# Expert products in exponential buffers, Gelus read from PSUM in even tiles, and the first group's Gelus in the attention's end

## The chip, the cores and the metric

The kernel runs on one core of one Trainium2 chip. The metric is the device time of the whole kernel in microseconds, the median of several runs. PE is the TensorE, DVE the VectorE, ACT the ScalarE, POOL the GpSimd engine, SP the engine that issues most DMAs.

## The reference

```python
x = L0_attn_x                                   # 16 x 512 x 128, f32
x = x + attn(layernorm(x), w_qkv, w_proj)       # 16 heads of 8, window +-128
x = x + ffn(layernorm(x), gamma, beta, w_q, keys, key_in, key_out)

def ffn(inputs, ...):                           # 8192 rows of 128
    xn = batchnorm(inputs) * gamma + beta
    q = xn @ w_q.T                              # 2 halves x 8 heads x 128
    sim = einsum('pbnhd,hkpd->pbnhk', q, keys)  # 2 x 8 heads x 32 keys
    # top 8 of each half, top 8 of their 64 sums: idx into 1024 experts, scores
    o = einsum('bnd,bnhkd->bnhk', inputs, key_in[idx])
    o = gelu(o, exact) * softmax(scores)
    return einsum('bnhk,bnhkd->bnd', o, key_out[idx])
```

## The kernel before

The program has two stages, one after the other, each with hand-written instruction streams for PE, DVE, ACT, POOL and SP that meet at semaphores. The first is the attention of 16 sequences with the layer norm after it; it writes x1 (the residual stream) and x2T (the normed rows, transposed) to DRAM and gathers the batch norm's statistics. The second is the FFN.

**FFN.** 8192 rows are 16 groups of four tiles of 128 rows; k is the tile in its group (0 to 3), so k = 0 and 2 are even tiles and k = 1 and 3 odd ones, and j counts all 64 tiles. The FFN doesn't gather experts. For each tile and each of 8 heads it builds all 1024 pair sums (POOL, L820, into a ring of 16 buffers SUM), takes the exponential of each less a bias (ACT, L947, into PSUM), masks with "at least the eighth best" (DVE, L1054, into W), and adds the transposed weights of the eight heads in the PSUM tile WT (PE, L1125, eight transposes a head). One head of a tile, LH = 3, goes another way: ACT shifts it (L903) and takes its exponential with the mask in it (L909), without DVE; it is called the log head below. Then DVE multiplies WT with the Gelus of the expert products (CT, L1034) and PE multiplies CT with key_out, the output product (L1086, L1089).

Exponentials have two PSUM buffers E of 128 x 1024: an exponential waits until the mask two before it is done. MB is one PSUM bank that passes between PE and ACT: the similarity product of tile j+3 (L1064, copied by ACT to SIM, L853), the output product of tile j-1 (copied to OUT, L873), and the expert products of the next group, key_in times X2T (L1067), two in a tile, each copied by ACT to GE (L864). Where the slots stand in the loop over heads h is set by SLOT_A, SLOT_OUT, SLOT_SIM, SLOT_B (PE) and COPY_B, COPY_A, COPY_OUT, COPY_SIM (ACT). After head 3 of tiles 2 and 0 ACT runs one Gelu over four products in GE (`gelus`, L859), with a table load before and one after (L859, L860).

The choice of the best eight of the next tile is DVE's small work, `choose`, in parts: 0 to 3 rank SIM's keys, 4 and 5 build and rank candidates, 6 is the sum Z of the small exponentials (L1007), 7 the biases NL and NB; 8 and 9 build the log head's pair sum on DVE for tiles 1 and 3. EVEN_PARTS and ODD_PARTS say which part stands before which head's mask. ACT adds `small_exp` (L890) after head 5, `small_ln` (L894) after head 6, and in tile 1 the batch-normed rows `bnt` (L868, before head 2's exponential).

At the FFN's start PE and ACT make the first group's eight expert products and Gelus (L1077, L881), with the first similarity product between them, and then the next two similarity products.

**Attention.** Step c works on the scores of sequence c, the exponentials of c-1, the values and projection of c-2, and the transposes of the second norm of c-3; each step is a loop over 16 heads. In step 17 (c == SEQS + 1) only the last values, the attention transposes (ASLOT, through MB one after the other), the projection and one X2T are left. MB's users come in the order of the list SHARED, and `bank_free` waits for the one before. SP's queue reloads x1 and x2T of sequence 0 for the FFN in step 17.

Of the kernel before, what the change touches and what calls it, by code (L numbers as in the profile page):

```python
# [52 lines left out]
def attention(nc, ctx, x, w_qkvT, w_projT, identb, band, bands, w_q, keysT, idf, bnst, KM, extra, x1_out, x2T_out, first):  # L53
# [6 lines left out]
    def sem(name):  # L60
# [56 lines left out]

    names = ("waits_passed max_parts_stored memory_loaded keys_merged keys_copied consts_loaded "
# [7 lines left out]
             "x1_stored x2T_stored x_stats x_means sums_inverted x1_stats x1_means first_loaded").split()  # L126
# [45 lines left out]
    def _(sp):  # L172
# [30 lines left out]
        def step(t, c):  # L203
            if 0 <= c - 2 < SEQS:
                if c - 3 >= 0:
                    await_(sp, S["x1_ready"], t - 2)
                sp.dma_start(xres[:, :, :], xs[t - 2]).then_inc(S["residual_loaded"], 16)
# [28 lines left out]
            if 0 <= c - 2 < SEQS:  # L236
                if c == SEQS + 1:
                    x1_first, x2T_first = first
                    sp.wait_ge(S["x1_stored"], 16)
                    sp.dma_start(x1_first[:, :, :], x1s[0]).then_inc(S["first_loaded"], 16)  # L240
                    sp.wait_ge(S["x2T_stored"], 16)
                    sp.dma_start(x2T_first[:, :], x2Ts[0]).then_inc(S["first_loaded"], 16)
                await_(sp, S["x1_ready"], t - 1)
                sp.dma_start(x1s[t - 2], X1[:, :, :]).then_inc(S["x1_stored"], 16)
# [53 lines left out]
    def _(act):  # L298
# [3 lines left out]
        def step(t, c):  # L302
            b = c % 2
            for h in range(H):
# [12 lines left out]
                if h == 3 and 0 <= c - 3 < SEQS:  # L317
# [79 lines left out]
    def _(dve):  # L397
# [41 lines left out]
        def step(t, c):  # L439
            b = c % 2  # L440
            for h in range(H):
# [58 lines left out]
                for i, sl in enumerate(ASLOT):  # L500
                    if h == sl and 0 <= c - 2 < SEQS:
                        n = (t - 2) * 2 + i + 1
                        dve.wait_ge(S["att_turned"], n)
                        hv = MB[:, :, :].rearrange("p g (h e) -> p (g h) e", e=SLOT_V // 2)
# [19 lines left out]
    def _(pe):  # L524
# [74 lines left out]
        def step(t, c):  # L599
            b = c % 2  # L600
            for h in range(H):
# [24 lines left out]
                if h == 3 and 0 <= c - 3 < SEQS:  # L626
# [24 lines left out]
                for i, sl in enumerate(ASLOT):  # L651
                    if h == sl and 0 <= c - 2 < SEQS:
                        bank_free(pe, f"att{i}", t, c)
                        pe.wait_ge(S["values_copied"], (t - 1) * 2)
                        for n in range(4):
                            k = 2 * i + n // 2
                            o = pe.transpose(MB[:, n, :], U[b][:, n % 2, k * P:(k + 1) * P], idf[:, :])
# [6 lines left out]
                if h == 14 and 0 <= c - 2 < SEQS:  # L664
# [3 lines left out]
                    o.then_inc(S["projected"], 1)  # L668

# [21 lines left out]
LH = 3  # L691
# [6 lines left out]
SIM0 = 2  # L698
SLOT_A, SLOT_OUT, SLOT_SIM, SLOT_B = 0, 2, 4, 6
COPY_B, COPY_A, COPY_OUT, COPY_SIM = 1, 3, 5, 7  # L700


def ffn(nc, ctx, x1, x2T, KM, key_in, key_out, gb, ident, bnst, first, out):
# [6 lines left out]
    def sem(name):  # L710
# [14 lines left out]
    GE = [sb(f"GE{b}", [P, BLK, GN]) for b in range(2)]  # L725
# [25 lines left out]
             "experts_weighted out_product out_copied expert_product expert_copied gelu_ready "  # L751
# [64 lines left out]

    def pair_sums(eng, j, h, q):
# [31 lines left out]
    def _(act):  # L849
# [26 lines left out]
        nc.scalar.preload_act_table_set("gelu_and_others")  # L876
        for e in range(BLK):
            if e == SIM0:
                sim_copy(0, 0)
            act.wait_ge(S["expert_product"], e + 1)  # L880
            nc.scalar.activation(GE[0][:, e, :], E[e // 2 % 2][:, e % 2 * GN:(e % 2 + 1) * GN], ACT.Gelu).then_inc(S["expert_copied"], 1)  # L881
        act.wait_ge(S["expert_copied"], BLK)
        act.sem_inc(S["gelu_ready"], 2)
        nc.scalar.preload_act_table_set("natural_log_exp_and_others")
        sim_copy(1, 1)
        sim_copy(2, 2)
# [27 lines left out]
        def group(g, b, more):  # L914
            for k in range(GT):
# [4 lines left out]
                for h in range(FH):  # L920
                    if h == 0:
                        act.wait_ge(S["bias_ready"], j + 1)

# [3 lines left out]
                    if h == COPY_B and k and more:  # L927
                        o_copy(g + 1, 1 - b, 2 * k - 1)
                    if h == COPY_B and not k and real:
                        o_copy(g, b, BLK - 1)  # L930
                    if h == COPY_A and more:
                        if k == 0:
                            wait_pos(act, S["experts_weighted"], g * GT)
                        o_copy(g + 1, 1 - b, 2 * k)
                    if h == COPY_OUT and (real or k):
# [17 lines left out]
                    if (k, h) == (2, 3) and more:  # L953
                        gelus(g + 1, 1 - b, 0)
                    if (k, h) == (0, 3) and real:
                        gelus(g, b, 1)
# [5 lines left out]
    def _(dve):  # L962
# [98 lines left out]
    def _(pe):  # L1061
# [4 lines left out]
        def o_block(b, e):  # L1066
# [123 lines left out]
```

## Time and profile before

| | us |
|---|---|
| median of three runs | 1676.41 (1676.0 to 1678.02) |
| the profiled execution | 1682.29 |
| its span, first to last instruction | 1680.5 |
| attention with its end | to about 715 |
| FFN | from about 715 to 1678 |

Spans and busy times are read as microseconds; a row of a timeline has start, duration, engine, line, operation, and in brackets the idle time of the engine before it and what ended it. Instructions of ACT and DVE that follow each other overlap by about 0.1 us, so a row of two is shorter than twice one.

### The profile page before, as it was taken

The page shows a single profiled execution, that of the slowest core. Times are in us where ns is not written, and L with a number is a line of the kernel's source. Part 1 is how long each engine was busy: PE and PEld are TensorE (multiplying, and loading weights), DVE is VectorE, ACT ScalarE, POOL GpSimd, SP SyncE. Part 2 cuts the span into 40 slices and gives each one's busy share as a digit, 9 for nine tenths or more (in the row PEclk, how much of TensorE's full clock was granted, in tenths as well). Part 3 has the DMA queues.
Part 4 walks back from the last instruction along what each step waited for, and adds up shares of the span by engine and source line. Part 5 has one row for each costly group of instructions (what it writes and reads, how often), then busy time and mean ns, then how long its engine had stood idle before and what let it go on. Part 6 is the DMA issues. An engine that isn't in the chain of part 4 may idle for free.

```text
span 1680.5 us, 33160 instructions
## 1 busy us (share of the span) xinstructions
PE 1473.9 (88%) x10688; PEld 1015.7 (60%) x10688; DVE 1477.5 (88%) x4616; ACT 1315.6 (78%) x1805; POOL 1269.8 (76%) x1547
## 2 busy tenths in 40 slices
PE   4799999999999999688888888888888888888887
PEld 2355555555555554356666767767676676767766
DVE  4789999999999996269999999999999999999997
ACT  1266666666666666479999999999999999999995
POOL 1055555556556555389999999999999999999992
PEclk7599999999999999789999999999999999999999
DMA  6344444554445551100000000000000000000000
GB/s 158 82 91 106 113 106 112 119 113 110 108 108 115 111 107 39 44 20 1 20 20 20 1 20 20 1 20 20 8 12 20 20 2 20 20 5 16 14 7 7
DMA packets 73629, 86.39 MB, mean 51 GB/s; under 512 B 9872, under 2 KB 63760, under 8 KB 68752
## 3 DMA queue, kind: packets, MB, share of 16 engines
q1 hardware_dynamic: 72840, 82.70, 20.7%
q10 hardware_dynamic: 616, 1.57, 0.5%
q8 instruction: 85, 1.39, 0.4%
q14 instruction: 88, 0.72, 0.2%
HBM read 58.30 MB, written 25.95 MB: 50 GB/s over the span
## 4 chain that ended last, share of the span: by engine, by line
ACT 21%; DVE 16%; PE 11%; issue 10%; DVEq 0%; ACTq 0%; SPq 0%
DVE W L1054 10%; ACT E L947 10%; PE WT L1125 7%; ACT L860 2%; ACT L859 2%; ACT W L909 2%; PE MB L1064 2%; PE MB L1067 2%; ACT SIM L853 1%; DVE SMALL L1000 1%; DVE M8Y L983 1%; ACT GE L859 1%; ACT GE L864 1%; PE E L1077 1%; DVE Z L1007 0%
## 5 line engine op out<-in xcount | busy, mean ns | idle before, releaser
L820 POOL TENSOR_TENSOR SUM<-SIM 128x1024 f32<-128x1024 f32 x480 | 899.5, 1910 | 34.2 <-DVE W L1054 30.8
L1125 PEld LDWEIGHTS WT<-idf,W 128*128 128x128 f32 x4096 | 478.6, 147 | 211.7 <-issue 126.4
L1054 DVE SCALAR_TENSOR_TENSOR W<-SUM,SMALL,E 128x1024 f32<-128x1024 f32 x448 | 560.6, 1280 | 42.6 <-ACT E L947 42.1
L1125 PE MATMUL WT<-idf,W 128*128 128x128 f32 x4096 | 545.4, 284 | 56.8 <-DVE CT L1034 38.0
L268 POOL TENSOR_SCALAR_AFFINE_SELECT PT<-PT 128x128 f32<-128x128 f32 (+1 forms) x1024 | 335.2, 353 | 266.5 <-ACT PT L371 230.8
L947 ACT ACTIVATE E<-SUM,NB 128x1024 f32<-128x1024 f32 x448 | 495.4, 1116 | 20.5 <-DVE W L1054 17.5
L430 DVE CUSTOM_DVE_ANT_0 SY<-SY,bandf 128x384 f32<-128x384 f32 x512 | 273.4, 574 | 0.0
L371 ACT ACTIVATE PT<-TX 128x512 f32<-128x512 f32 x256 | 153.1, 598 | 116.3 <-PE TX L565 116.1
L451 DVE TENSOR_REDUCE mx<-SX 128x2 f32<-128x512 f32 x256 | 174.6, 682 | 58.9 <-PE SX L547 58.8
L373 ACT ACTIVATE PT<-TY 128x768 f32<-128x768 f32 x256 | 207.6, 811 | 4.1 <-PE TY L565 0.4
L593 PE MATMUL PV<-PT,V 128*32 128x384 f32 (+1 forms) x2048 | 166.8, 444 | 2.6 <-POOL PT L268 2.4
L537 PE MATMUL SY<-K,Q 72*128 72x384 bf16 x512 | 145.1, 342 | 8.6 <-DVE mx L430 4.7
L1064 PE MATMUL MB<-KM,BNT 128*128 128x512 f32 x128 | 76.7, 683 | 72.7 <-ACT OUT L873 70.9
L565 PE MATMUL TY<-Q,K 75*128 75x384 bf16 x512 | 128.3, 333 | 11.3 <-ACT PT L373 10.2
L1089 PE MATMUL MB<-KO,CT 128*128 128x128 f32 x1024 | 124.9, 275 | 1.1 <-DVE CT L1034 1.1
L537 PE MATMUL SX<-K,Q 72*128 72x256 bf16 x512 | 103.0, 283 | 19.9 <-issue 9.3
L1089 PEld LDWEIGHTS MB<-KO,CT 128*128 128x128 f32 x1024 | 119.5, 192 | 1.3 <-DVE CT L1034 1.3
L565 PE MATMUL TX<-Q,K 75*128 75x256 bf16 x512 | 101.3, 280 | 2.4 <-ACT PT L371 2.0
L565 PEld LDWEIGHTS TX<-Q,K 75*128 75x128 bf16 x512 | 38.4, 99 | 97.7 <-issue 84.0
L593 PEld LDWEIGHTS PV<-PT,V 128*32 128x32 f32 x2048 | 53.8, 110 | 68.8 <-issue 50.0
L1034 DVE TENSOR_TENSOR CT<-WT,GE 128x1024 f32<-128x1024 f32 x64 | 78.4, 1225 | 12.7 <-PE WT L1125 12.7
L537 PEld LDWEIGHTS SX<-K,Q 72*128 72x128 bf16 x512 | 49.2, 100 | 63.3 <-DVE mx L451 14.6
(121 smaller groups left out, 1858.6 us busy)
## 6 DMA issues: line engine op xcount, KB each, us to landing
Q<-q_parts SPq DMA_DIRECT2D x288, 64.0 KB
K<-k_parts SPq DMA_DIRECT2D x90, 192.0 KB
q_parts<-qp SPq DMA_DIRECT2D x16, 384.0 KB, 2.4
k_parts<-kp SPq DMA_DIRECT2D x15, 384.0 KB, 2.4
xin<-in_x SPq DMA_DIRECT2D x16, 256.0 KB, 3.2
xres<-in_x SPq DMA_DIRECT2D x16, 256.0 KB, 9.5
x<-X SPq DMA_DIRECT2D x16, 256.0 KB, 2.2
x2T<-X2T SPq DMA_DIRECT2D x16, 256.0 KB, 2.1
```

The costliest lines, as they stand in the source:

```text
L268: return nc.gpsimd.affine_select(out=out, in_=out, compare_op=ALU.is_ge, fill=0.0, base=0, pattern=([[0, 2]] if pairs else []) + [[s, P]], ...
L373: nc.scalar.activation(pt[:, 512:1280].rearrange("p (j n) -> p j n", j=2), TY[:, :, 0:384], ACT.Exp).then_inc(S["inner_exp"], 1)
L430: return nc.vector.tensor_tensor_reduce(out=scores, in0=scores, in1=bandf[:, k0 * P:k1 * P], scale=1.0, scalar=-3e38, op0=ALU.add, op1=ALU ...
L451: nc.vector.tensor_reduce(mx[:, h, 0:4:3], SX[:, :, :], AX.X, ALU.max).then_inc(S["outer_maxima"], 1)
L537: return pe.matmul(out, Q[b][0:KQ, h, i * P:(i + 1) * P], K[b][0:KQ, h, k0 * P:k1 * P], start=clear, stop=done, skip_group_check=True)
L565: return pe.matmul(out[:, 0:(q1 - q0) * P], K[b][0:R, h, j * P:(j + 1) * P], Q[b][0:R, h, q0 * P:q1 * P], start=True, stop=True, skip_grou ...
L593: o = pe.matmul(PV[32 * e:32 * e + 32, q0 * P:q1 * P], V[b][:, slot:slot + SLOT_V], PT[:, h % 8, at:at + (q1 - q0) * P], start=(j == 0 and ...
L820: return eng.tensor_tensor(SUM[(q * FH + h) % RING][:, :].rearrange("p (i j) -> p i j", i=NK), sx, sy, ALU.add)
L947: nc.scalar.activation(E[(n - 1) % 2][:, :], SUM[(k * FH + h) % RING][:, :], ACT.Exp, bias=NB[q][:, h:h + 1]).then_inc(S["exp_ready"], 1)
L1054: nc.vector.scalar_tensor_tensor(out=W[h % WRING][:, :], in0=SUM[(k * FH + h) % RING][:, :], scalar=TOP[q][:, h, TOPK - 1:TOPK], in1=E[(n ...
L1089: o = pe.matmul(po, CT[k % 2][:, e, :], key_out[:, e, :], start=False, stop=(e == BLK - 1))
L1125: o = pe.matmul(WT[:, e, :], W[h % WRING][:, e * P:(e + 1) * P], ident[:, :], is_transpose=True, start=(h == 0 and e % 4 == 0), stop=(h == ...
```

## The change

- **Expert products.** They leave MB. In the even tiles, four products at a time go into the two exponential buffers (`expert_bank`), a pair after mask 0 and a pair after mask 1, and ACT's Gelu reads them from PSUM, one by one, and writes GE. The copies L864 are gone. k = 2 makes the first four of the next group, k = 0 the last four of its own.
- **Order in a tile.** The log head is 2 instead of 3. The output product stands at head 2 in even tiles and at head 0 in odd ones (SLOT_OUT), its copy at 4 and 5. The small work moves to before mask 3 in even tiles and from head 4 to head 5 (parts 4 and 5) in odd ones.
- **The first group.** Its eight products and Gelus move to step 17 of the attention, into the score buffers SY and TY, at heads 0, 9 and 14. For that the loads of sequence 0 move to step 16 on SP, the X2T transposes and copy of step 17 move from head 3 to 8, and the second attention transposes go to SX, right behind the first.

```diff
+    def first_bank(e):
+        return (SY if e // 2 % 2 == 0 else TY)[:, e % 2, :]
+    def att_bank(i, c):
+        return SX[:, :, :].rearrange("p j (i n) -> p (j i) n", n=P) if i == 1 and c == SEQS + 1 else MB[:, :, :]
+    FIRST = ((0, 0, 2), (9, 2, 4), (14, 4, 8))
...
         def step(t, c):
+            if c == SEQS:
+                sp.wait_ge(S["x1_stored"], 16)
+                sp.dma_start(first[0][:, :, :], x1s[0]).then_inc(S["first_loaded"], 16)
+                sp.wait_ge(S["x2T_stored"], 16)
+                sp.dma_start(first[1][:, :], x2Ts[0]).then_inc(S["first_loaded"], 16)
...
-                if h == 3 and 0 <= c - 3 < SEQS:
+                if h == (8 if c == SEQS + 1 else 3) and 0 <= c - 3 < SEQS:
...
+                for hh, e0, e1 in FIRST:
+                    if h == hh and c == SEQS + 1:
+                        if e0 == 0:
+                            nc.scalar.preload_act_table_set("gelu_and_others")
+                        for e in range(e0, e1):
+                            act.wait_ge(S["first_product"], e + 1)
+                            nc.scalar.activation(first[2][:, e, :], first_bank(e), ACT.Gelu).then_inc(S["first_gelu"], 1)
...
-                    if h == sl and 0 <= c - 2 < SEQS:
-                        bank_free(pe, f"att{i}", t, c)
+                    if h == (ASLOT[0] if c == SEQS + 1 else sl) and 0 <= c - 2 < SEQS:
+                        if i == 1 and c == SEQS + 1:
+                            pe.wait_ge(S["outer_maxima"], SEQS * H)
+                        else:
+                            bank_free(pe, f"att{i}", t, c)
...
+                for hh, e0, e1 in FIRST:
+                    if h == hh and c == SEQS + 1:
+                        pe.wait_ge(S["first_loaded"], 32)
...
+                        for e in range(e0, e1):
+                            if e >= 4:
+                                pe.wait_ge(S["first_gelu"], e - 3)
+                            pe.matmul(first_bank(e), first[3][:, e * P:(e + 1) * P], first[1][:, :], start=True, stop=True).then_inc(S["first_product"], 1)
...
-LH = 3
+LH = 2
-EVEN_PARTS = ((), (), (), (), ((1, 0), (1, 1), (1, 2), (1, 3), (1, 4), (1, 5), (1, 8), (2, 0), (2, 1), (1, 9)), (), ((1, 6),), ((1, 7),))
-ODD_PARTS = ((), (), ((1, 2),), ((1, 3),), ((1, 4), (1, 5)), (), ((1, 6),), ((1, 7),))
-SLOT_A, SLOT_OUT, SLOT_SIM, SLOT_B = 0, 2, 4, 6
-COPY_B, COPY_A, COPY_OUT, COPY_SIM = 1, 3, 5, 7
+EVEN_PARTS = ((), (), (), ((1, 0), (1, 1), (1, 2), (1, 3), (1, 4), (1, 5), (1, 8), (2, 0), (2, 1), (1, 9)), (), (), ((1, 6),), ((1, 7),))
+ODD_PARTS = ((), (), ((1, 2),), (), ((1, 3),), ((1, 4), (1, 5)), ((1, 6),), ((1, 7),))
+SLOT_OUT, SLOT_SIM = (2, 0), 4
+COPY_OUT, COPY_SIM = (4, 5), 7
...
+    def expert_bank(j, e):
+        return E[(j * MASKED + e // 2) % 2][:, e % 2 * GN:(e % 2 + 1) * GN]
...
-        def gelus(g, b, half):
-            act.wait_ge(S["expert_copied"], g * BLK + (half + 1) * 4)
-            o = GE[b][:, 4 * half:4 * half + 4, :].rearrange("p e n -> p (e n)")
-            nc.scalar.activation(o, o, ACT.Gelu).then_inc(S["gelu_ready"], 1)
+        def gelus(j, g, b, half):
+            wait_pos(act, S["experts_weighted"], (g - 1) * GT)
+            nc.scalar.preload_act_table_set("gelu_and_others")
+            for e in range(4 * half, 4 * half + 4):
+                act.wait_ge(S["expert_product"], g * BLK + e + 1)
+                nc.scalar.activation(GE[b][:, e, :], expert_bank(j, e), ACT.Gelu).then_inc(S["expert_copied"], 1)
             nc.scalar.preload_act_table_set("natural_log_exp_and_others")
+            act.wait_ge(S["expert_copied"], g * BLK + 4 * half + 4)
...
+        def o_blocks(j, g, b, half, h):
+            if half == 0:
+                pe.wait_ge(S["x2T_loaded"], (g + 1) * 16)
+            pe.wait_ge(S["weights_masked"], masked(j, h))
+            for e in range(4 * half + 2 * h, 4 * half + 2 * h + 2):
+                pe.matmul(expert_bank(j, e), key_in[:, e * P:(e + 1) * P], X2T[b][:, :], start=True, stop=True).then_inc(S["expert_product"], 1)
...
                 for h in range(FH):
+                    for hh, after in ((0, 0), (2, 1)):
+                        if h == hh and k == 2 and more:
+                            o_blocks(j, g + 1, 1 - b, 0, after)
+                        if h == hh and k == 0 and real:
+                            o_blocks(j, g, b, 1, after)
-                    if h == SLOT_OUT and real:
+                    if h == SLOT_OUT[k % 2] and real:
```

## Rows read from the trace of the kernel before

**Rows 1.** Busy us (count) by stretch: PE, PEld, DVE, ACT, POOL; PE's granted clock.
```profile
728.50:1678.00 949.50, 819.77 (x5610) 657.73 (x5610) 876.64 (x2658) 878.71 (x1055) 890.95 (x476) 0.96 0.04 13
1002.45:1061.62 59.17, 51.37 (x355) 41.08 (x354) 55.00 (x170) 55.77 (x67) 57.36 (x32) 0.97 0.05 14
1066.30:1069.70 3.40, 3.39 (x11) 2.21 (x12) 3.40 (x4) 3.21 (x6) 2.33 (x2) 0.53 0.01 2
694.30:697.50 3.20, 3.17 (x20) 1.31 (x20) 1.11 (x4) 0.00 (x0) 0.94 (x1) 0.51 0.15 44
```

**Rows 2.** Groups of instructions from 720 us to the end, costliest first.
```profile
L820 POOL TENSOR_TENSOR SUM<-SIM 128x1024 f32<-128x1024 f32 x480 | 899.5, 1910 | 34.2 <-DVE W L1054 30.8 <-ACT SIM L853 3.2
...
L864 ACT COPY GE<-MB 128x512 f32<-128x512 f32 x120 | 70.0, 583 | 6.4 <-PE MB L1067 6.4
...
L859 ACT ACTIVATE GE<-GE 128x2048 f32<-128x2048 f32 x30 | 57.5, 1916 | 0.3
...
L881 ACT ACTIVATE GE<-E 128x512 f32<-128x512 f32 x6 | 3.6, 597 | 1.6 <-PE E L1077 1.6
```

**Rows 3.** DVE in order of time, one even and one odd tile.
```profile
1024.81 2.48 DVE L1054 SCALAR_TENSOR_TENSOR W<-SUM,SMALL,E 128x1024 f32<-128x1024 f32 x2 [0.37 <-ACT E L947]
1027.29 1.23 DVE L1034 TENSOR_TENSOR CT<-WT,GE 128x1024 f32<-128x1024 f32 x1
...
1030.81 0.85 DVE L983 MAX8 SMALL<-SIM 128x8 f32<-128x32 f32 x8
...
1036.67 2.49 DVE L1054 SCALAR_TENSOR_TENSOR W<-SUM,SMALL,E 128x1024 f32<-128x1024 f32 x2 [0.53 <-ACT E L947]
1039.08 0.21 DVE L1007 TENSOR_REDUCE Z<-E 128x8 f32<-128x64 f32 x1
...
1041.07 2.48 DVE L1054 SCALAR_TENSOR_TENSOR W<-SUM,SMALL,E 128x1024 f32<-128x1024 f32 x2 [0.38 <-ACT E L947]
...
1048.11 0.22 DVE L990 TENSOR_TENSOR CD<-SMALL,M8Y 128x64 f32<-128x64 f32 x1
...
1049.77 2.47 DVE L1054 SCALAR_TENSOR_TENSOR W<-SUM,SMALL,E 128x1024 f32<-128x1024 f32 x2
...
1054.14 1.29 DVE L1054 SCALAR_TENSOR_TENSOR W<-SUM,SMALL,E 128x1024 f32<-128x1024 f32 x1 [0.37 <-ACT E L947]
```

**Rows 4.** ACT in order of time, the same two tiles.
```profile
1029.83 1.15 ACT L909 ACTIVATE W<-SUM,NL 128x1024 f32<-128x1024 f32 x1
1031.00 1.28 ACT L859 ACT_TABLE_LOAD   x1
...
1034.22 1.28 ACT L860 ACT_TABLE_LOAD   x1
1035.52 1.12 ACT L947 ACTIVATE E<-SUM,NB 128x1024 f32<-128x1024 f32 x1
...
1039.91 2.16 ACT L947 ACTIVATE E<-SUM,NB 128x1024 f32<-128x1024 f32 x2
...
1043.52 0.81 ACT L868 ACTIVATE BNT<-X2T_first,ab 128x512 f32<-128x512 f32 x1
```

**Rows 5.** Line 1007 over the FFN, one Z for each tile.
```profile
L1007 DVE TENSOR_REDUCE Z<-E x64: 210/211/220, 729.0 to 1658.3; 128x8 f32<-128x64 f32 x64
```

**Rows 6.** PE in order of time, in two even tiles.
```profile
1011.57 1.02 PE L1067 MATMUL MB<-X2T,KI 128*128 128x512 f32 x2
1012.43 1.91 PE L1125 MATMUL WT<-idf,W 128*128 128x128 f32 x16
...
1066.31 2.04 PE L1064 MATMUL MB<-KM,BNT 128*128 128x512 f32 x2 [2.37 <-ACT OUT L873]
```

**Rows 7.** The attention's end and the FFN's start in order of time.
```profile
698.95 0.59 ACT L356 COPY U<-PV 128x512 f32<-128x512 f32 x1 [0.66 <-PE PV L593]
...
719.32 0.58 ACT L853 COPY SIM<-MB 128x512 f32<-128x512 f32 x1 [0.26 <-PE MB L1064]
...
729.85 2.15 ACT L947 ACTIVATE E<-SUM,NB 128x1024 f32<-128x1024 f32 x2 [0.35 <-DVE NB L1011]
```

More of the change, by code:

```diff
@@ L236, in step @@
             if 0 <= c - 2 < SEQS:
[L237 to L242, printed above, removed]
                 await_(sp, S["x1_ready"], t - 1)
@@ L625, in step @@
                     o.then_inc(S["xn_turned"], 1)
-                if h == 3 and 0 <= c - 3 < SEQS:
+                if h == (8 if c == SEQS + 1 else 3) and 0 <= c - 3 < SEQS:
                     bank_free(pe, "x2T", t, c)
@@ L724, in ffn @@
     BNT = [sb(f"BNT{b}", [P, GN]) for b in range(2)]
-    GE = [sb(f"GE{b}", [P, BLK, GN]) for b in range(2)]
+    GE = [first[2], sb("GE1", [P, BLK, GN])]
     OUT = [sb(f"OUT{b}", [P, GT, P]) for b in range(2)]
@@ L873, in finish @@
             nc.scalar.copy(OUT[b][:, k, :], MB[:, 0:P]).then_inc(S["out_copied"], 1)
[L876 to L883, printed above, removed]
+        act.sem_inc(S["expert_copied"], BLK)
         nc.scalar.preload_act_table_set("natural_log_exp_and_others")
+        sim_copy(0, 0)
         sim_copy(1, 1)
-        sim_copy(2, 2)
         def small_exp(j):
@@ L922, in group @@
                         act.wait_ge(S["bias_ready"], j + 1)
+                    if h == 1 and j == 0:
+                        sim_copy(2, 2)
                     if h == 2 and k == 1 and more:
                         bnt(g + 1, 1 - b)
[L927 to L935, printed above, removed]
+                    if h == COPY_OUT[k % 2] and (real or k):
                         finish(j - 1, *((g, b, k - 1) if k else (g - 1, 1 - b, GT - 1)))
@@ L942, in group @@
                         l_exp(j, k, q)
+                        if k == 2 and more:
+                            gelus(j, g + 1, 1 - b, 0)
+                        if k == 0 and real:
+                            gelus(j, g, b, 1)
                     else:
@@ L952, in group @@
                         small_ln(j + 1)
[L953 to L956, printed above, removed]
         steps(act, group)
@@ L1064, in similar @@
             pe.matmul(MB[:, :], BNT[b][:, k * P:(k + 1) * P], KM[:, :], start=True, stop=True).then_inc(S["sim_product"], 1)
-        def o_block(b, e):
-            pe.matmul(MB[:, :], key_in[:, e * P:(e + 1) * P], X2T[b][:, :], start=True, stop=True).then_inc(S["expert_product"], 1)
-        for e in range(BLK):
-            if e == SIM0:
-                pe.wait_ge(S["bn_rows"], 1)
-                similar(0, 0, 0)
-            pe.wait_ge(S["x2T_loaded"], 16)
-            if e >= 4:
-                pe.wait_ge(S["expert_copied"], e - 3)
-            pe.matmul(E[e // 2 % 2][:, e % 2 * GN:(e % 2 + 1) * GN], key_in[:, e * P:(e + 1) * P], X2T[0][:, :],
-                      start=True, stop=True).then_inc(S["expert_product"], 1)
-        for k in (1, 2):
-            pe.wait_ge(S["sim_copied"], k)
+        def o_blocks(j, g, b, half, h):
[4 more added lines that the diff above has]
+                pe.matmul(expert_bank(j, e), key_in[:, e * P:(e + 1) * P], X2T[b][:, :], start=True, stop=True).then_inc(S["expert_product"], 1)
+        pe.sem_inc(S["expert_product"], BLK)
+        pe.wait_ge(S["bn_rows"], 1)
+        for k in range(3):
+            if k:
+                pe.wait_ge(S["sim_copied"], k)
             similar(k, 0, k)
@@ L1096, in group @@
                 for h in range(FH):
-                    if h == SLOT_A and more:
-                        pe.wait_ge(S["x2T_loaded"], (g + 2) * 16)
-                        pe.wait_ge(S["sim_copied"], j + 3)
-                        pe.wait_ge(S["expert_copied"], (g + 1) * BLK + 2 * k)
-                        o_block(1 - b, 2 * k)
-                    if h == SLOT_OUT and real:
+                    for hh, after in ((0, 0), (2, 1)):
[4 more added lines that the diff above has]
+                    if h == SLOT_OUT[k % 2] and real:
                         pe.wait_ge(S["sim_copied"], j + 3 if more or k < 2 else GROUPS * GT)
-                        pe.wait_ge(S["expert_copied"], (g + 1) * BLK + (2 * k + 1 if more else 0))
                         wait_pos(pe, S["out_copied"], j - 1)
@@ L1109, in group @@
                         pe.wait_ge(S["bn_rows"], (g + 1) if k < 1 else (g + 2))
-                        pe.wait_ge(S["expert_copied"], (g + 1) * BLK + (2 * k + 1 if more else 0))
                         wait_pos(pe, S["out_copied"], j)
                         similar(j + 3, b if k < 1 else 1 - b, (k + 3) % GT)
-                    if h == SLOT_B and more:
-                        pe.wait_ge(S["sim_copied"], j + 4)
-                        o_block(1 - b, 2 * k + 1)
                     if h == LH:
@@ L1146, in program @@
         bnst = sb("bnst", [P, SEQS, 6])
-        first = [sb("X1_first", [P, TILES, P]), sb("X2T_first", [P, T])]
+        first = [sb("X1_first", [P, TILES, P]), sb("X2T_first", [P, T]), sb("GE_first", [P, BLK, T]), KI]
         extra = [(idf[:, :], ident), (KI[:, :], key_inT), (KO[:, :, :], key_out), (GB[:, :], gb)]
```

19 lines of the change are left out of this document (10 added, 9 removed).

## The prediction

> **What bounds the kernel now.** I read the busy times by stretch first. Over the FFN, ACT is busy 879 us, DVE 877, POOL 891 and PE 820 of 949.5; in one period of four tiles (59.17 us) ACT is busy 55.8, DVE 55.0 and PE 51.4 [rows 1]. No engine is full, so the waits between them count. POOL makes 30 pair sums in a period (480 in 16), 1.874 us each (899.5 / 480), so 56.2 us: a floor that no saving on ACT can pass [rows 2].
>
> Then I read one even and one odd tile in order of time. Both are measured from M, the start of the mask of head 7 of the tile before. The even tile runs from M = 1024.81 to 1041.07 (16.26 us), the odd one to 1054.14 (13.07) [rows 3]. In the even tile ACT runs without a gap: the log head's exponential at M+5.02, table load M+6.19, Gelu, table load back M+9.41, exponential M+10.71 [rows 4]. DVE, which has its small operations from M+6.00 to M+11.33, waits 0.53 us for that exponential [rows 3]. Then Z starts at 1039.08, and from Z to the next mask of head 7 it is always 1.99 us (log, copy of SIM, exponential), in either kind of tile. From the first Z to the last it is 63 tiles in 929.3 us [rows 5]. 29 of the even tiles take 16.25 to 16.50, the other three 13.92, 15.77 and 14.55; that leaves 929.3 - 44.2 - 471.5 = 413.6 for 31 odd tiles, 13.34 each.
>
> **What leaves ACT.** Eight copies of 0.583 go, and two Gelus of 1.916 become eight of 0.597 [rows 2]. A copy and the next instruction overlap by 0.10, so one copy is 0.48 of ACT's time and one small Gelu 0.49: 8 x 0.48 + 2 x 1.92 - 8 x 0.49 = 3.8 us per period off ACT. The table loads stay four, 1.28 each [rows 4]. ACT had 3.4 us of gaps in a period already [rows 1], so the saving counts only where ACT is late for DVE. That is the even tile.
>
> **The even tile, worked out.** Exponential 7 starts at M-1.16, since the mask needs it. Exponentials follow each other by 1.04 (two in 2.16 [rows 4]): exponential 0 M-0.12, shift M+0.92, exponential 1 M+1.96, log head M+3.00, table load M+4.17, first Gelu M+5.47. Two copies and one exponential fewer stand before it, so four Gelus without a wait would end at M+7.6 and exponential 3 would be done at M+10.0.
> But the Gelus now wait for PE. A product is 0.86 of PE (two records in 1.02, the next starts 0.86 after), a head's eight transposes are 0.87 [rows 6]. Mask 0 starts at M+1.19 and lasts 1.28, so pair 0 starts on PE at M+2.6 and holds it to M+4.33. CT takes M+2.47 to M+3.70 and doesn't delay that. Transposes of head 0 end at M+5.20, those of head 1 at M+6.07. Only then, in head 2's slot, come the other two products: the first is there at M+7.09, the second at M+7.95. The third Gelu waits 0.6, the fourth 0.4; the last ends at M+8.58, the load at M+9.88, exponential 3 at M+11.02, and mask 3 starts at M+11.05. DVE's small work (5.33 from M+4.76) was done at M+10.09: a stall of 0.96 where 0.53 stood.
> After it come three masks instead of two, since the log head is now head 2. Mask 4 at M+12.26; exponential 5 needs mask 3 finished (M+12.33, and 0.1 to pass it on), so mask 5 starts 0.12 late; Z at M+14.77, next M 1.99 later: 16.76. That is +0.50 on 16.26. Behind pair 1 on PE are the output product (to M+10.1) and head 2's transposes; the output copy on ACT at M+12 and mask 3 hide both.
>
> **The odd tiles.** Output product first: PE starts it at CT's end, M+3.75, to M+5.8, then heads 0 to 3 to M+9.3 and the similarity. ACT's output copy stands at head 5 (M+6.1), and nobody waits. With no bnt (k = 3): exponential 3 is done at M+5.16, DVE is ready at M+5.23; mask 3, part 3 (0.50), mask 4 at M+6.92, parts 4 and 5 (1.66, 1048.11 to 1049.77 [rows 3]), mask 5, Z at M+10.96, so 12.95. No expert product stands before head 7's transposes now, so CT doesn't come late. That was the difference between 13.07 and the mean of 13.34. So -0.39. With bnt (k = 1) ACT has 0.71 more (0.81, overlapping) between exponential 1 and the log head [rows 4]; before, the 1.66 of small work lay across the log head and covered it, now that work comes after mask 4. Exponential 3 is done at M+5.87, DVE was ready at M+5.23, and the tile is 13.63: +0.29. Cover gone: 0.68.
>
> Steady part: 30 even tiles x 0.50 = 15.0, 15 tiles k = 1 x 0.29 = 4.4, 16 tiles k = 3 x -0.39 = -6.2: **+13.2 us**. Bounds: the even tile between 15.8 (no wait for products at all, -0.5) and 17.8 (a slow PE, below).
>
> **The beginning of the FFN.** Before, the first exponential starts at 729.85, because ACT has eight Gelus between SIM's first copy (719.32) and its third [rows 7]. Without them: the similarity product runs on a PE that idled before, and I give it 0.8 more, so SIM's copy ends at 720.7 (719.90 before); DVE's choice is 3.4 of the 5.33 us of small work (no parts 8 and 9, nothing of tile 2); the small exponential and what lies from Z (729.0) to the first exponential take 1.15; it starts at 725.25. **-4.6**. POOL starts 0.8 later. At 1.874 a sum its first sum is there 2.6 us before the first exponential and, through the small work of each even tile, keeps ahead.
>
> **The attention's end.** From 694.30 to 697.50 ACT has nothing to do [rows 1]; the Gelu table load and the first two Gelus, 2.5 us, lie mostly there, and their products in PE's pause just ahead. X2's transposes no longer stand between the two halves of the last values, so U's copy (698.95 [rows 7]) comes up to 2 us earlier, and the two attention transposes no longer wait for each other through MB. Against this, products 2 and 3 stand before A's transposes (1.7 at full clock, 3.4 at half) and four more before the last X2 transposes (3.4 or 6.9). At 2.4 GHz I get 2.6 us less, at 1.2 GHz 2.0 more. The trace has PE at 0.51 just there [rows 1]; between them I take **-1.0**. The two loads that move into an earlier step on SP wait on stores of sequence 0, long landed, and hold up nothing in that queue.
>
> **The sum.** 13.2 - 4.6 - 1.0 = +7.6 us. The profiled execution took 1682.29 us (span 1680.5, 1.8 around it) and would be 1689.9; it is 5.9 above the median of the runs, 1676.41, so I predict **1684 us**.
>
> **A rule on the clock.** Before, PE idles 2.37 us in the even tile before the similarity product, which then takes 2.04 instead of 1.02; the granted clock of the next 3.4 us is 0.53, that is mostly 1.2 GHz [rows 1, 6]. In the new order the idle time is some 1.4 us before head 3, and less elsewhere, so I take full speed in my sum.
> The Trainium skill (TensorE: Matmul & The Clock Gate, "HAM oscillation — how this bites in real kernels") says that idle gaps between bursts of matmuls send the clock back to half, and that the gaps are what to remove. By it the shorter gaps help; the trace agrees in that the slow stretch follows the gap, but the attention shows the low clock after less idling, so it doesn't settle the matter.
>
> **Rivals.**
> - *The second pair is in time (faster, 1664).* If the last product were there at M+7.0 instead of 7.95, mask 3 would start at M+10.1, and the even tile would be 15.8: 30 x -0.45 = -13.5, with the rest (4.4 - 6.2 - 5.6) -20.9, so 1656; halfway, 1667. It decides at M+7.45, where the even tile is as long as before. For it: ACT loses 3.8 us of work per period. Against it: PE must do both heads' transposes first, 1.74 us that the rows price well.
> The Trainium skill (Perfetto Trace Analysis, "Matmuls") asks that products rotate through PSUM banks so that their evacuation overlaps the next ones, which this change does; that rule would have it faster, with this rival's 1667.
> - *The clock falls in the even tile (slower still).* The similarity product now follows mask 3 and head 3's transposes, to M+14.2 at full speed; ACT copies it at M+15.0. At 1.2 GHz both take double, 1.7 more in all: ready at M+16.1, and the tile is 1.0 longer. In two even tiles of three, 20 us more: 1704.
> - *Nothing measurable.* With PE's handoffs 0.1 quicker than I took, the attention's end at -2.6, and k = 3 as worked out: 30 x 0.35 + 4.4 - 6.2 - 7.2 = +1.5, 1678.
>
> **Chances.** Forecast 0.45, clock 0.17, nothing 0.15, faster rival 0.23. This kernel's measurement tells about 0.2% (3.4 us) from no change. Faster 0.23, same 0.15, slower 0.62. The range reaches into the faster rival and short of the clock's full price: 1664 to 1700; the forecast's own is 1680 to 1690.
>
> **What would show it.** In an even tile: two ACT waits on line E's expert product before the third and fourth Gelu, some 0.6 and 0.4; DVE's wait before mask 3 near 0.96; Z to Z near 16.75. Odd tiles 12.95 and 13.63, with a DVE wait of 0.7 in the second alone. First exponential of the FFN 4 to 5 us sooner after X2T's last copy. ACT's busy time in a period about 3.8 less, POOL with more waits. The prediction fails if the second pair's products start before M+5.5, if a low clock falls on the pairs (then Gelus wait up to 3 us), or if PE's clock in the attention's end differs.

## The result

The changed kernel takes 1681.68 us (median of 11 runs, 1678.94 to 1687.40), the kernel before 1676.41 (median of 11 runs): a ratio of 1.0036, 95% interval 1.0023 to 1.0049, so 4 to 8 us slower. The prediction said 1684. Its profiled execution has a span of 1681.4.

The busy times by stretch of the changed kernel, to be read beside [rows 1]: the whole FFN, one period of four tiles, and 3.4 us of an odd tile.

```profile
718.50:1678.00 959.50, 798.79 (x5609) 651.75 (x5609) 877.52 (x2656) 828.77 (x1022) 894.41 (x478) 0.98 0.04 13
1015.67:1075.61 59.94, 51.05 (x346) 42.45 (x344) 55.12 (x169) 52.56 (x66) 56.20 (x31) 0.94 0.05 14
1038.20:1041.60 3.40, 3.39 (x16) 3.39 (x17) 2.78 (x7) 3.16 (x4) 3.40 (x3) 0.50 0.00 0
```

ACT lost 50 us of work over the FFN (828.8 against 878.7), 3.2 in the period. The period still grew from 59.17 to 59.94. Its groups of instructions from 715 us on, beside [rows 2]:

```profile
L856 POOL TENSOR_TENSOR SUM<-SIM 128x1024 f32<-128x1024 f32 x480 | 898.8, 1917 | 44.3 <-DVE W L1076 40.3 <-ACT SIM L889 4.0
L1076 DVE SCALAR_TENSOR_TENSOR W<-SUM,SMALL,E 128x1024 f32<-128x1024 f32 x448 | 565.8, 1280 | 65.6 <-ACT E L973 63.8
...
L897 ACT ACTIVATE GE<-E 128x512 f32<-128x512 f32 x64 | 36.5, 596 | 14.7 <-PE E L1094 14.5
...
L897 ACT ACTIVATE GE_first<-E 128x512 f32<-128x512 f32 x56 | 31.9, 596 | 12.9 <-PE E L1094 12.7
...
L918 ACT ACTIVATE E<-D 128x64 f32<-128x64 f32 x64 | 15.9, 248 | 59.4 <-DVE D L1025 59.4
```

The Gelus cost what was taken for them (596 ns), and ACT now waits 27.2 us for PE's products before them. POOL's waits rose from 34.2 to 44.3. The freed time of ACT turned up as waits: 59.4 us before the small exponential alone, where it had waited 1.0 us in the kernel before.

ACT in an even tile, in order of time, beside [rows 4]:

```profile
1021.83 1.28 ACT L894 ACT_TABLE_LOAD   x1
1023.12 1.09 ACT L897 ACTIVATE GE<-E 128x512 f32<-128x512 f32 x2
1024.82 0.60 ACT L897 ACTIVATE GE<-E 128x512 f32<-128x512 f32 x1 [0.61 <-PE E L1094]
1025.68 0.60 ACT L897 ACTIVATE GE<-E 128x512 f32<-128x512 f32 x1 [0.26 <-PE E L1094]
1026.29 1.28 ACT L898 ACT_TABLE_LOAD   x1
1027.59 1.12 ACT L973 ACTIVATE E<-SUM,NB 128x1024 f32<-128x1024 f32 x1
```

PE in the same tile and the following odd one:

```profile
1022.01 1.91 PE L1141 MATMUL WT<-idf,W 128*128 128x128 f32 x16
1023.76 1.88 PE L1094 MATMUL E<-X2T,KI 128*128 128x512 f32 x4
...
1038.21 3.67 PE L1110 MATMUL MB<-KO,CT 128*128 128x128 f32 x16 [1.09 <-DVE CT L1056]
```

DVE in both tiles, beside [rows 3]:

```profile
1028.74 3.82 DVE L1076 SCALAR_TENSOR_TENSOR W<-SUM,SMALL,E 128x1024 f32<-128x1024 f32 x3 [0.96 <-ACT E L973]
1032.47 0.21 DVE L1029 TENSOR_REDUCE Z<-E 128x8 f32<-128x64 f32 x1
...
1034.46 2.48 DVE L1076 SCALAR_TENSOR_TENSOR W<-SUM,SMALL,E 128x1024 f32<-128x1024 f32 x2 [0.38 <-ACT E L973]
...
1040.35 1.28 DVE L1076 SCALAR_TENSOR_TENSOR W<-SUM,SMALL,E 128x1024 f32<-128x1024 f32 x1 [0.62 <-ACT E L973]
...
1045.96 0.21 DVE L1029 TENSOR_REDUCE Z<-E 128x8 f32<-128x64 f32 x1
```

These rows show the even tile's chain: both heads' transposes hold PE until 1023.76, then comes the second pair; the third Gelu waits 0.61, the fourth 0.26; and DVE waits 0.96 before mask 3. In the odd tile k = 1, DVE waits 0.62. From Z to Z nearly all even tiles take 16.80 to 16.87 us (16.25 before), the odd ones with k = 1 13.49 and those with k = 3 12.79. PE's low clock in the rows above (0.50 from 1038.2) is not in every odd tile: behind the same wait of 1.09 us for CT the granted clock fell in 4 of the 31 and was 1.00 in the others.

The line of Z over the FFN, beside [rows 5]:

```profile
L1029 DVE TENSOR_REDUCE Z<-E x64: 209/211/220, 717.8 to 1660.5; 128x8 f32<-128x64 f32 x64
```

First to last Z is 942.8 us where it was 929.3: +13.5. In front of it the FFN's start and the attention's end are shorter. The changed kernel, beside [rows 7]:

```profile
689.08 0.81 ACT L391 ACTIVATE PT<-TY 128x768 f32<-128x768 f32 x1
...
693.30 0.58 ACT L366 COPY U<-PV 128x512 f32<-128x512 f32 x1 [1.01 <-PE PV L611]
...
705.27 0.58 ACT L332 COPY X2T<-MB 128x512 f32<-128x512 f32 x1 [1.34 <-PE MB L648]
...
718.58 1.12 ACT L973 ACTIVATE E<-SUM,NB 128x1024 f32<-128x1024 f32 x1 [0.35 <-DVE NB L1033]
```

The two lines of the kernel before that this needs:

```profile
692.54 0.81 ACT L373 ACTIVATE PT<-TY 128x768 f32<-128x768 f32 x1
...
711.92 0.58 ACT L322 COPY X2T<-MB 128x512 f32<-128x512 f32 x1 [7.86 <-PE MB L630]
```

From the attention's last exponential to X2T's last copy: 16.19 us for 19.38, -3.2. From there to the FFN's first exponential: 13.31 for 17.93, -4.6. Behind the last Z the span has 20.8 left for 22.2, -1.4; what shortened it was not traced. These and the +13.5 make +4.3, inside the interval. The two profiled spans differ by only 0.9, because in this execution of the kernel before the attention up to its last exponential happened to take 3.5 us more, in code that the change doesn't touch; the medians are the better measure.

### The profile page after: what moved, and what is told of

Read it like the earlier page. It is cut to its first block, busy times and chain, and to the rows that moved or that the text cites. A ratio compares the mean times of both kernels' runs of the same rounds, so it can differ in the third digit from the quotient of the medians.

```text
span 1681.4 us, 33023 instructions
## 1 busy us (share of the span) xinstructions
PE 1448.0 (86%) x10688; PEld 1007.8 (60%) x10688; DVE 1478.5 (88%) x4616; ACT 1265.7 (75%) x1775; POOL 1269.3 (75%) x1547
## 4 chain that ended last, share of the span: by engine, by line
POOL 13%; issue 13%; DVE 12%; ACT 10%; PE 9%; DVEq 0%; DMA 0%; ACTq 0%; SPq 0%
POOL SUM L856 13%; DVE W L1076 8%; ACT E L973 7%; PE E L1094 5%; PE WT L1141 3%; ACT SIM L889 2%; DVE SMALL L1022 1%; DVE M8Y L1005 1%; ACT W L937 1%; DVE Z L1029 1%; ACT BNT L903 0%; PE MB L1110 0%; DVE CT L1056 0%; DVE NT L1026 0%; ACT SUM L931 0%
## 5 line engine op out<-in xcount | busy, mean ns | idle before, releaser
L856 POOL TENSOR_TENSOR SUM<-SIM 128x1024 f32<-128x1024 f32 x480 | 898.8, 1917 | 44.3 <-DVE W L1076 40.3
L1141 PE MATMUL WT<-idf,W 128*128 128x128 f32 x4096 | 516.5, 277 | 120.2 <-DVE W L1076 118.3
L1141 PEld LDWEIGHTS WT<-idf,W 128*128 128x128 f32 x4096 | 457.4, 142 | 212.4 <-DVE W L1076 167.9
L1110 PE MATMUL MB<-KO,CT 128*128 128x128 f32 x1024 | 134.4, 287 | 36.1 <-DVE CT L1056 36.1
L1110 PEld LDWEIGHTS MB<-KO,CT 128*128 128x128 f32 x1024 | 125.3, 200 | 42.4 <-DVE CT L1056 42.4
L555 PEld LDWEIGHTS SY<-K,Q 72*128 72x128 bf16 x512 | 51.0, 100 | 50.3 <-DVE mx L448 43.2
L1086 PE MATMUL MB<-KM,BNT 128*128 128x512 f32 x128 | 69.6, 626 | 7.4 <-DVE BNT L1047 6.1
```

The costliest lines, as they stand in the source:

```text
L555: return pe.matmul(out, Q[b][0:KQ, h, i * P:(i + 1) * P], K[b][0:KQ, h, k0 * P:k1 * P], start=clear, stop=done, skip_group_check=True)
L856: return eng.tensor_tensor(SUM[(q * FH + h) % RING][:, :].rearrange("p (i j) -> p i j", i=NK), sx, sy, ALU.add)
L1110: o = pe.matmul(po, CT[k % 2][:, e, :], key_out[:, e, :], start=False, stop=(e == BLK - 1))
L1141: o = pe.matmul(WT[:, e, :], W[h % WRING][:, e * P:(e + 1) * P], ident[:, :], is_transpose=True, start=(h == 0 and e % 4 == 0), stop=(h == ...
```

## The experiments

Line numbers below are those of the changed kernel where the edit keeps them. Each kernel was timed beside the kernel before (medians 1676.4 to 1677.4). The attention is the same code in the changed kernel and in all the experiments, and still the first Z came anywhere from 711.8 to 721.5 us in their profiled executions. So the stretch from the first to the last Z shows what an edit did to the FFN's loop more sharply than the whole time does:

| kernel | first to last Z, us | less the changed kernel's |
|---|---|---|
| before | 929.2 | -13.5 |
| changed | 942.8 | |
| 1, second pair earlier | 917.1 | -25.7 |
| 2, second pair later | 1018.5 | +75.7 |
| 3, odd tiles' small work as before | 939.4 | -3.3 |
| 4, output product at head 2 | 961.8 | +19.0 |
| 5, experiment 4 with the gap filled | 943.1 | +0.3 |
| 6, only the first group moved | 930.5 | -12.3 |
| 7, experiments 1 and 3 together | 912.8 | -30.0 |
| 8, experiment 7 with SIM's copy moved | 896.1 | -46.7 |

**1. The second pair one slot earlier.** Theory: PE's order sets the even tile. Rival: the small Gelus and the third mask do.

```diff
-                    for hh, after in ((0, 0), (2, 1)):
+                    for hh, after in ((0, 0), (1, 1)):
```

> The changed kernel with one edit: the second pair of expert products stands ahead of head 1's transposes on PE instead of ahead of head 2's. Theory (the even tile's end is set by PE's order: the third and fourth Gelu wait 0.61 and 0.26 us for the second pair): both products come 0.87 us earlier, exponential 3 is done at M+10.17, DVE is ready at M+10.10, so the stall before mask 3 falls from 0.96 to about 0.1 and the even tile from 16.80-16.87 to 15.95 us; 30 tiles, 26 us less than the changed kernel, about 1655 us. Rival (the even tile is longer because three masks follow the table load instead of two, and because four small Gelus cost more than one): the tile stays above 16.7 and the time within 3 us of 1682.

1656.21 us, ratio to before 0.9869 (0.9847 to 0.9892): 25.5 us less than the changed kernel. Nearly all even tiles take 15.93 to 16.00, the odd ones are unchanged. ACT, then DVE in an even tile of this kernel:

```profile
1016.89 2.28 ACT L897 ACTIVATE GE<-E 128x512 f32<-128x512 f32 x4
```

```profile
1021.64 3.82 DVE L1076 SCALAR_TENSOR_TENSOR W<-SUM,SMALL,E 128x1024 f32<-128x1024 f32 x3
```

All four Gelus run as one piece here, and DVE has no wait worth a bracket before mask 3. The rival has fallen: the same Gelus, loads and three masks stand in this kernel.

**2. The second pair later.**

```diff
-                    for hh, after in ((0, 0), (2, 1)):
+                    for hh, after in ((0, 0),):
...
                         outputs(j - 1, ...)
+                    for hh, after in ((2, 1),):
+                        ... o_blocks(...)            # the same two calls
```

> The changed kernel with the second pair moved the other way, behind the output product in head 2's slot. The output product holds PE for 2.0 us. Theory: each even tile is longer by these 2.0 us (18.8), 60 us in 30 tiles, about 1742 us, and ACT's wait before the third Gelu is 2.6 instead of 0.61. Rival (PE's order isn't what sets the tile): less than 5 us.

1755.85 us, ratio 1.0459 (1.0430 to 1.0487): 74 us more than the changed kernel. The even tiles are 18.82 to 18.88, longer by the 2.0 expected, 60 us in all. Of the rest, 12 us are in the odd tiles with k = 3, most of them 13.6 where they were 12.79, and 4 us in the first five with k = 1 (14.06 to 14.57). ACT, DVE and PE in an even tile with k = 2, and PE in the next even tile:

```profile
1017.01 0.60 ACT L897 ACTIVATE GE<-E 128x512 f32<-128x512 f32 x1 [2.69 <-PE E L1094]
...
1025.85 0.59 ACT L889 COPY SIM<-MB 128x512 f32<-128x512 f32 x1 [0.73 <-PE MB L1086]
```

```profile
1020.93 3.82 DVE L1076 SCALAR_TENSOR_TENSOR W<-SUM,SMALL,E 128x1024 f32<-128x1024 f32 x3 [3.03 <-ACT E L973]
...
1027.49 2.48 DVE L1076 SCALAR_TENSOR_TENSOR W<-SUM,SMALL,E 128x1024 f32<-128x1024 f32 x2 [1.23 <-ACT E L973]
```

```profile
1022.27 1.97 PE L1146 MATMUL WT<-idf,W 128*128 128x128 f32 x8 [3.57 <-DVE W L1076]
1024.03 1.78 PE L1086 MATMUL MB<-KM,BNT 128*128 128x512 f32 x2
...
1054.72 1.09 PE L1146 MATMUL WT<-idf,W 128*128 128x128 f32 x8 [3.57 <-DVE W L1076]
```

The 2.0 us pass one to one from PE through ACT to DVE. PE idles 3.57 us here, and then eight transposes take 1.97 instead of 1.09: the granted clock is 0.57 from 1022 to 1026. The similarity product is late by it, its copy waits 0.73, and DVE waits 1.23 for exponential 7 where it waits 0.35 to 0.39 at full clock: these 0.85 us are what the odd tile that follows has more (13.64). That is the clock rival of the prediction, at work in this kernel, with its price in the odd tile that follows. A gap of this length didn't always bring it: behind 3.57 us the clock fell in every even tile with k = 2, but from 1050 us on it stayed full in 9 of the 11 with k = 0.

**3. The odd tiles' small work as before.**

```diff
-ODD_PARTS = ((), (), ((1, 2),), (), ((1, 3),), ((1, 4), (1, 5)), ((1, 6),), ((1, 7),))
+ODD_PARTS = ((), (), ((1, 2),), ((1, 3),), ((1, 4), (1, 5)), (), ((1, 6),), ((1, 7),))
```

> The changed kernel with DVE's small work of the odd tiles where it was before the change: part 3 ahead of head 3's mask, parts 4 and 5 ahead of head 4's. Theory (in tiles k = 1 bnt puts ACT's exponential 3 behind DVE, and small work moved away had covered it): the tiles k = 1 go from 13.49 to 12.95, those with k = 3 stay at 12.79, DVE's wait before mask 3 falls from 0.62 to below 0.2; 15 tiles, 8 us less than the changed kernel, about 1674 us. Rival (the k = 1 tiles are longer for PE's half clock at the output product): no change, 1682 us.

1676.21 us, ratio 0.9993 (0.9976 to 1.0009), 5.5 us less than the changed kernel. Tiles k = 1 are 13.13, k = 3 12.77, nearly all of them. Mask 3 in a tile k = 1:

```profile
1042.72 1.28 DVE L1076 SCALAR_TENSOR_TENSOR W<-SUM,SMALL,E 128x1024 f32<-128x1024 f32 x1 [0.26 <-ACT E L973]
```

0.36 of the 0.62 us went: part 3 alone now covers for bnt, and its 0.4 us is all that it can cover. The direction is right, the size was expected at 8 us. In the profiled execution five even tiles took 17.2 and two 17.5 instead of 16.8, each behind an odd tile in which the granted clock fell at the wait for CT; this cost 2.6 us, and the loop gained only 3.3 there. The rival falls too: in the changed kernel the tiles k = 1 are 13.49 with the clock at 0.50 behind the wait for CT as with it at 1.00.

**4. The output product of the odd tiles back at head 2.**

```diff
-SLOT_OUT, SLOT_SIM = (2, 0), 4
+SLOT_OUT, SLOT_SIM = (2, 2), 4
```

> The changed kernel with the output product of the odd tiles back at head 2 on PE (its copy stays at head 5 on ACT). Theory (nobody waits for the output product in an odd tile): PE transposes heads 0 and 1 first, the product ends at about M+7.5 instead of 5.8, ACT copies it before exponential 5, which is done some 1 us before DVE needs it; odd tiles stay at 13.49 and 12.79, within 3 us of the changed kernel, about 1682 us. Rival (output first is what shortened the odd tiles with k = 3 from 13.34 to 12.79): those grow by 0.5, 8 us more, 1690 us.

1701.90 us, ratio 1.0146 (1.0124 to 1.0168), 20 us more than the changed kernel. Both sides of the expectation missed: from 910 us on the odd tiles are 13.9, k = 1 and k = 3 alike; before that those with k = 3 are 12.79 and those with k = 1 13.5 to 13.6, but for the first. PE, its granted clock over that stretch, ACT and DVE:

```profile
1039.58 3.51 PE L1141 MATMUL WT<-idf,W 128*128 128x128 f32 x16 [1.41 <-DVE CT L1056]
1042.93 0.39 PE L1107 MATMUL MB<-X,idf 128*128 128x128 f32 x2
```

```profile
1039.58:1043.00 3.42, 3.42 (x17) 3.42 (x18) 2.80 (x8) 3.06 (x3) 3.42 (x3) 0.53 0.00 0
```

```profile
1045.14 0.27 ACT L908 COPY OUT<-MB 128x128 f32<-128x128 f32 x1 [2.50 <-PE MB L1110]
```

```profile
1046.46 1.29 DVE L1076 SCALAR_TENSOR_TENSOR W<-SUM,SMALL,E 128x1024 f32<-128x1024 f32 x1 [0.33 <-ACT E L973]
```

After PE's wait for CT the granted clock is 0.53, so mostly 1.2 GHz; two heads' transposes take 3.51 instead of 1.91, the output product ends 1.6 us later than counted, ACT waits 2.50 for it ahead of exponential 5, and mask 5 waits 0.33 (1.0 in the tiles k = 3). Behind this gap of 1.41 us the granted clock was 1.00 in the first six odd tiles and 0.51 to 0.56 in each of the 25 from 916 us on: the long tiles are the ones with the low clock.

**5. The gap filled.** If it is the clock, needless work in PE's gap must make the kernel of experiment 4 faster. The edit stands on top of experiment 4's.

```diff
+                    if h == 0 and k % 2:
+                        pe.wait_ge(S["sim_copied"], j + 3 if more or k < 2 else GROUPS * GT)
+                        wait_pos(pe, S["out_copied"], j - 1)
+                        for _ in range(2):
+                            pe.matmul(MB[:, :], ident[:, :], KM[:, :], start=True, stop=True)
                     if h == SLOT_OUT[k % 2] and real:
```

> The kernel with the output product at head 2 in odd tiles (1702 us; odd tiles 13.88), plus two idle products of 128 x 512 into MB ahead of head 0's transposes in odd tiles, where PE otherwise waits 1.41 us for CT. Their result is overwritten by the output product; they are work that isn't needed. Theory (odd tiles are long there because after this gap the transposes of heads 0 and 1 run at half clock, 3.51 instead of 1.91 us, so the output product and its copy come 1.6 late): with the gap filled the granted clock stays near 1, the transposes take 1.91, the output copy waits 0.9 less or more, and the odd tiles fall to 13.5 and 12.8, 20 us less, about 1682 us, in spite of 1.7 us more PE work in each. Rival (only the order counts, not the clock): PE has more work before the copy and the odd tiles get longer, 1702 us or more.

1682.63 us, ratio 1.0034 (1.0019 to 1.0050): 19 us less than the kernel of experiment 4, with 55 us more work on PE. The odd tiles are 13.49 and 12.79 again, those of the changed kernel, and from the filled gap on the granted clock is 1.00 in all 31 of them. PE and ACT in an odd tile:

```profile
1034.16 1.88 PE L1128 MATMUL MB<-KM,idf 128*128 128x512 f32 x4
1035.88 2.04 PE L1146 MATMUL WT<-idf,W 128*128 128x128 f32 x16
```

```profile
1039.97 0.27 ACT L908 COPY OUT<-MB 128x128 f32<-128x128 f32 x1 [1.18 <-PE MB L1110]
```

The transposes behind the filled gap take 2.04. The order alone would have made this kernel no faster.

**6. The kernel before with only the first group moved.** The FFN's loop is that of before; the edit is the change's part in the attention's steps 16 and 17, GE_first, and the FFN's start without products and Gelus.

> The kernel before with only the first group's products and Gelus moved into the attention's end (with the moved loads, X2T transposes and the second attention transposes in SX); the FFN's tiles are those of before. Theory: the attention's end 3.2 us and the FFN's start 4.6 us shorter, nothing else changes: 7.8 us less than before, ratio 0.9953, about 1668.6 us. Rival (the earlier start is given back, because POOL has less of a lead on the first tiles): within 2 us of before.

1669.27 us, ratio 0.9947 (0.9925 to 0.9968): 5 to 13 us less than before, 7.8 was expected. The seam is that of the changed kernel: 16.20 us from the attention's last exponential to X2T's last copy and 13.34 from there to the FFN's first exponential. So the change is a gain of 7 to 8 us at the seam and a loss of 12 in the loop (1681.7 less 1669.3), which the prediction had at 13.2.

**7. Both gains together.** The edits of experiments 1 and 3.

> The changed kernel with both edits that gained by themselves: second pair ahead of head 1's transposes, and the odd tiles' small work as before. Theory (the two waits lie in different tiles, so they add): even tiles 15.93 to 16.00, k = 1 13.13, k = 3 12.77, a period of 57.8 us; 25.5 + 5.5 us less than the changed kernel, about 1650 us. Rival (POOL, whose floor is 56.2 us a period, begins to set the time): a gain under 28 us, and ACT or DVE waits that end with POOL's sums.

1651.98 us, ratio 0.9843 (0.9820 to 0.9866), 29.7 less than the changed kernel; 31 were expected. Most even tiles take 15.93 to 16.00 (five of them 16.3), k = 1 13.12, k = 3 12.77.

**8. SIM's copy behind exponential 6.** The wait that stood in nearly every tile of all these kernels, 0.35 to 0.39 before the mask of head 7, goes through the small log, the copy and exponential 7 on ACT. The edit stands on top of experiment 7's.

```diff
-                    if h == COPY_SIM and (more or k < 1):
-                        sim_copy(j + 3, (k + 3) % 4)
...                                                   # behind exponential h:
+                    if h == 6 and (more or k < 1):
+                        sim_copy(j + 3, (k + 3) % 4)
                     if h == 6 and nxt:
                         small_ln(j + 1)
```

> The kernel with both edits, and ACT's copy of the similarity product moved from ahead of exponential 7 to behind exponential 6, ahead of the small log. There ACT waits 0.27 us for Z in even tiles and 0.13 in odd ones, and the 0.47 of the copy lie between the log and exponential 7, for which DVE waits 0.35 to 0.39 in every tile. Theory: the copy fills those waits, exponential 7 comes 0.31 earlier in even tiles and 0.19 in odd ones, a period of 56.8, 16 us less than with the two edits, about 1634 us. Rival (the similarity product isn't there yet, or POOL's floor of 56.2 us a period with its uneven demand holds the tiles): less than 6 us, with an ACT wait on the similarity product or on SUM.

1631.29 us, ratio 0.9724 (0.9706 to 0.9742), 20.7 less than the kernel of experiment 7, where 16 were expected. Nearly all even tiles take 15.71 to 15.77, k = 1 12.89, k = 3 12.42, a period of 56.8. The loop from first to last Z lost 16.8 us, as expected; in the profiled executions another 7.3 lie before the first Z, in code that the edit doesn't touch, so the edit itself is worth nearer 17 than 21. ACT in an even tile, and POOL from 740 to 1600 us:

```profile
1040.39 0.58 ACT L889 COPY SIM<-MB 128x512 f32<-128x512 f32 x1
1040.87 0.21 ACT L922 ACTIVATE LZ<-Z 128x8 f32<-128x8 f32 x1
1040.97 1.11 ACT L971 ACTIVATE E<-SUM,NB 128x1024 f32<-128x1024 f32 x1
```

```profile
L856 POOL TENSOR_TENSOR SUM<-SIM 128x1024 f32<-128x1024 f32 x460 | 860.6, 1913 | 0.0
```

The log no longer waits for Z, exponential 7 follows it at once, and POOL has no idle time in this stretch, in which it is still getting ahead of ACT (460 sums, 454 are used up in 860 us). The kernel stands 0.6 us a period above the floor of 56.2 that the pair sums set. This is the fastest version, 45 us below the kernel before.

## Why the prediction was right

**The even tile**, +0.50 forecast: +0.58 measured (16.83 for 16.25). Its mechanism held link by link: waits of 0.61 and 0.26 before the last two Gelus (0.6 and 0.4 said), 0.96 before mask 3 (0.96 said). Experiments 1 and 2 moved only PE's order and got -0.87 and +2.0 a tile. The term was a little too small all the same: 29 of the even tiles grew by 17.3 us together, 0.1 a tile more than forecast, and the three short ones that the prediction listed apart, at the FFN's two ends, added another 2.0.

**The odd tiles.** k = 3: 12.79, 12.95 said; k = 1: 13.49, 13.63 said, with the wait of 0.62 in it (0.68 said). Both are 0.15 shorter than counted; 0.10 of it is part 3, which costs 0.40 between two masks and not 0.50. Added up over the FFN, by kind of tile: even +19.3 (15.0 said), k = 1 +2.0 (4.4), k = 3 -7.7 (-6.2), in all +13.5 against 13.2. The total was closer than its terms, whose errors went both ways.

**The FFN's start:** -4.6 as said; the similarity product took 2.07 on a PE that had idled, for which 0.8 more had been allowed. **The attention's end:** -3.2, where -1.0 was taken and -2.6 was the best case. There the term was mis-sized: PE was given the middle between its two clock levels, but the granted clock is 1.00 from 688.5 to 705.3, where it was 0.72 from 692 to 712 before, and the last projection takes 1.16 us where it took 1.94. The first two expert products now stand in PE's pause; that they are what kept the clock up was not tested alone, and the 0.6 us beyond the best case were not traced. The 1.4 us behind the last Z were not in the sum.

**What was right for an incomplete reason.** The prediction put the difference between 13.07 and the mean of 13.34 down to an expert product that stood before head 7's transposes and made CT late. The trace of the kernel before shows that this took the low clock as well. PE's granted clock behind the gap before the similarity product of an even tile, and CT in the two odd tiles that follow such a gap at full clock and at the lower level ([rows 1] and [rows 6] have the gap and the clock before the second; the gap before the first is 2.37 us too):

```profile
1036.90:1040.30 3.40, 3.21 (x19) 2.23 (x20) 3.40 (x4) 3.21 (x6) 2.27 (x2) 1.00 0.27 77
```

```profile
1043.54 1.23 DVE L1034 TENSOR_TENSOR CT<-WT,GE 128x1024 f32<-128x1024 f32 x1
...
1073.37 1.23 DVE L1034 TENSOR_TENSOR CT<-WT,GE 128x1024 f32<-128x1024 f32 x1 [0.49 <-PE WT L1125]
```

Of the first 30 even tiles, the clock fell in 19, and in each odd tile behind them CT waited 0.46 to 0.75 us; behind the 11 at full clock CT never waited and the odd tiles took 12.90 to 13.10, with the same expert product in its old place. One odd tile behind a fallen clock had no expert product (in the last group) and didn't wait either, so the wait seems to need both. Against odd tiles at full clock, then, k = 3 gains only 0.1 us and k = 1 loses 0.42; against the mean of 13.34 they come out as 0.55 less and 0.15 more. The waits of CT in these 19 tiles were 11.6 us together. In the changed kernel the clock stays up in the even tiles and the product has moved as well; whether one of the two would have been enough was not tried.

"In an odd tile nobody waits for the output product" held for nearly all of the changed kernel. The sum had PE at full clock in the loop; in 4 of 31 odd tiles it was near 0.50 for 3.4 us right behind the wait for CT, and the output product took 3.67 instead of 1.95. ACT then waited 0.55 to 1.26 for it, and only one tile was longer by it, the even one behind it (17.49). Experiments 4 and 5 show what would have hung on it: with the product at head 2 and the low clock 20 us, and with the product at the same place and the gap filled nothing, though ACT then waits 1.18 for it. Experiment 4 has no expert product before head 7's transposes either and gives 13.9 in the tiles k = 3, so their gain also needs the early output product or PE's full clock.

**The rivals.** That the second pair is in time didn't happen in the changed kernel; experiment 1 built it: 1656 us, where the rival had 1656 for all of it. The clock didn't fall in the changed kernel's even tiles, but for the very first; it does in experiment 2. The Trainium skill's rule on gaps (TensorE: Matmul & The Clock Gate, "HAM oscillation — how this bites in real kernels"), by which idle gaps between bursts of matmuls bring the clock back to half, could not be settled from the trace of before. Here the traces agree with it in part: filling a gap of 1.4 us took 19 us off, but behind the same 3.57 us of experiment 2 the clock fell in some tiles and stayed full in others. The Trainium skill's advice that products rotate through banks (Perfetto Trace Analysis, "Matmuls") pays off only where the order on PE lets it: the changed kernel follows it and is slower, experiment 1 follows it too and is faster.

## What to carry to other kernels

When a copy or an operation is taken off an engine that looks full, trace the next wait of the engine behind it: here the work left ACT, and the tile's end passed to two products that stood one slot too late on PE, 25 us for one number. A product that another engine is about to read belongs ahead of transposes that nobody awaits yet, and small independent work belongs where the other engine is late, not evenly. Put what is awaited first behind a gap of PE, or fill the gap, for what follows it may run at half clock. And before a mean over tiles is taken as a base, the tiles that make it up should be sorted by PE's clock: here it hid two kinds.

## What the runs showed of the hardware that was not expected

Two products of 128 x 512 without use, 1.7 us of PE in each odd tile, made a kernel 19 us faster: behind a gap of 1.4 us 16 transposes took 3.51 us, behind the filled one 2.04. A gap's length alone doesn't tell whether the clock falls behind it. Behind 1.41 us in experiment 4 it stayed full in the first six odd tiles and fell in all 25 that followed; behind 1.09 us in the changed kernel it fell in 4 of 31; behind 1.56 us in that kernel's even tiles it never fell; behind 2.37 us in the kernel before it fell in two even tiles of three, and behind 3.57 us in experiment 2 in some. What PE did before the gap, or when the gap came, must matter too, and what exactly decides was not tried.
